# Row sums of x on ScalarE (copies with an accumulator) instead of VectorE, from the third batch on

## The chip, the cores and the metric

The kernel runs on one core of one Trainium2 chip. The metric is the device time of one execution in microseconds; the median of three executions of the kernel before is 617.11 us.

## The reference

A graph attention over 16 batches of 512 nodes with 512 features, two directions (d = 0, 1), 16 heads of 32, and only the first 20 nodes as keys:

```
row_zero = v.sum(-1) == 0                       # per node
q_exp = where(row_zero, 0, q)                   # query features only for nonzero rows
self_feat = concat(v, q_exp) @ W_self.T + b_self
for d in 0, 1:
    A = adj (or its transpose), first 20 keys
    aff = (self_feat Wq)(kv Wk) / sqrt(32), masked where A sums to 0, + A @ w_bias + b_bias
    output += softmax(aff) @ kv, then Wout per head
out = v + relu(output)
```

The change concerns `v.sum(-1)` alone: one sum of 512 float32 values for each of the 512 rows of a batch. The other thing that the sums feed is the test for zero.

## The kernel before

Each engine has its program written out by hand, and semaphores order them. The host gives x twice: `x` with features on partitions, and `xn` with nodes on partitions (512 rows as 128 partitions of 4 rows). For a batch n = b + 1 (next batch) the work is pipelined into batch b:

- SyncE loads `xn`, two rows per partition at a time (`load_rows(b, half)`, 128x1024 values, one buffer), and stores and reloads the zero test as a broadcast row (`store_nonzero`, `load_nonzero`). The row sums run two batches ahead: in batch b they are those of batch b + 2. `load_rows(b + 2, 1)` waits until the first half's sums are done, since there is only one buffer; behind it in SyncE's queue stand `load_c`, `load_x`, `load_mask`, `store_nonzero`, `load_rows(b + 3, 0)` and `load_nonzero`.
- VectorE reduces each half to two columns of `rsum` (`row_sums`, L926 to L928), and `nonzero` (L930 to L934) turns the four sums of a partition into 0 or 1.
- TensorE, per batch: `scores` for four tiles of 128 nodes (L572), `self_feat` of the next batch (L500 to L502, results in PSUM `gen`), the transposes of the softmax weights in five chunks (L584: chunks 0 and 1, then the last `self_feat`, then chunks 2, 3, 4), `attend_rest` (L629) and `attend` 0 to 3 (L500 to L502 into `aff`). In the batches 1, 4, 7, 10 and 13 it also makes the key products of the next group (L540) between the `self_feat` parts. Transposes 2 wait for `wt_low(0)`, transposes 3 for `wt_low(1)`, `attend_rest` for the last `g_low`, the next batch's `scores` for `add_sf(0)` and `add_sf(1)`.
- ScalarE, per batch: `x_high` (L707), the label products (L720) and edge terms (L712 to L716) interleaved with the exp of the four tiles (L880), `sf_high` (L725), in the batches 1, 4, 7, 10, 13 `evict_g` (L737), `evict_wt` of the five chunks (L742), `relu` (L746).
- VectorE, per batch: label sums (L984), `row_sums`, `shift` of each tile (L994, L996), `total` (L1009, L1011), `add_query` (L940), `g_low` (L951) in the batches 1, 4, 7, 10, 13, `row_sums`, `wt_low` 0 and 1 (L956), `nonzero`, `add_query(3)`, `wt_low` 2 to 4, `add_sf` 0 and 1 (L978), `sf_low` (L945), `add_sf` 2 and 3.
- GpSimd, per batch: `x_low` (L1279), `sub_max` (L1298), `normalise_rest` and `normalise` (L1302, L1310), `sf_low` of three chunks (L1283), `bias` of the next batch (L1286, four instructions), and the DMA that adds x to the output (L1321).

"Batch 10" below is the pass of all engines with b = 10. The last use of `row_sums` is in batch 13.

Of the kernel before, what the change touches and what calls it, by code (L numbers as in the profile page):

```python
# [10 lines left out]
ACT = mybir.ActivationFunctionType  # L11
# [34 lines left out]
def build(nc, B, a, out):  # L46
# [4 lines left out]
    with ExitStack() as ctx:  # L51
        def sb(name, shape, dt=F32, stack=ctx):
            return stack.enter_context(nc.sbuf_tensor(name, shape, dt))

        def sem(name):
            return ctx.enter_context(nc.semaphore(name))
# [20 lines left out]
        xn = sb("xn", [P, 2, F])  # L77
        rsum, nzc = sb("rsum", [P, T]), sb("nzc", [P, T])
# [15 lines left out]
        def slots(*held):  # L94
            made = {}
            for k in range(max(len(h) for h in held)):
                with ExitStack() as own:
                    for n, h in enumerate(held):
# [74 lines left out]
        s_xn0, s_xnin, s_rsum, s_nzc, s_nzst, s_nzin = (sem("rows0_in"), sem("rows_in"), sem("row_sums"), sem("nonzero_rows"), sem("nonzero_stored"),  # L173
                                                 sem("nonzero_in"))
# [62 lines left out]
        def upto(b, c):  # L237

            return chunk(b, (LAST_ORDER.index(c) if b == B - 1 else c) + 1)
# [463 lines left out]
        def _(act):  # L703
            def x_high(n):
                act.wait_ge(s_xin, n * 16 + 16)
                for c in range(FC):
                    nc.scalar.activation(xh[:, c, :], x[:, c, :], ACT.Copy).then_inc(s_xh, 1)  # L707

            def edge_terms(n):

                act.wait_ge(s_cond, n + 1)
                nc.scalar.activation(cond[:], cond[:], ACT.Relu).then_inc(s_neg, 1)  # L712
                act.wait_ge(s_neg, n * 3 + 1)
                nc.scalar.activation(cond[:], cond[:], ACT.Relu, scale=-1.0, bias=one[:, 0:1]).then_inc(s_neg, 1)
                act.wait_ge(s_neg, n * 3 + 2)
                nc.scalar.activation(prod[:, :, :, L], cond[:], ACT.Identity, scale=NEG, bias=wb[:, L:L + 1]).then_inc(s_neg, 1)  # L716
# [23 lines left out]
            def evict_wt(b, slot, c):  # L740
                act.wait_ge(s_tp, upto(b, c))
                nc.scalar.activation(wt_high(c), wt_bank(b, c), ACT.Copy).then_inc(s_wth, 1)  # L742
# [114 lines left out]
            def batch(b, slot, i, ahead):  # L857
                n, other = b + 1, 1 - slot
                next_g, pair = next_group(b) is not None, next_group(b)
                if next_g:  # L860
                    k_blocks(pair)
                if ahead >= 1 and b > 0:
                    act.wait_ge(s_sf, b * FC + FC)
                    x_high(n)
                if ahead == 2 and b > 0:
                    act.wait_ge(s_mskin, b * 16 + 48)
                    act.wait_ge(s_vred, b * D + 2 * D)
                    labels(b + 2, range(0, L, LG))
                if ahead == 0:
                    for j in range(HG):  # L870
                        add_bosum(b, slot, j)
                for t in range(T):
                    if next_g and t == T - 1:
                        evict_g(pair, 0)
                        evict_g(pair, 1)
                    if ahead == 0 and t == T - 1:
                        act.wait_ge(s_sub3, 1)
                    else:
                        act.wait_ge(s_sub, b * T + (t + 1))
                    nc.scalar.activation(z[slot][:, t, :], z[slot][:, t, :], ACT.Exp).then_inc(s_exp, 1)  # L880
                    if b == 0 and t == 0:
                        edge_terms(1)
                    if ahead == 2 and b > 0 and t + 1 < LG:
                        labels(b + 2, range(t + 1, L, LG))
                    if ahead == 2 and b > 0 and t + 1 == LG:
                        edge_terms(b + 2)
                if b == 0:
                    act.wait_ge(s_mskin, 48)
                    act.wait_ge(s_vred, 2 * D)
                    labels(2, range(0, L, LG))  # L890
                    sf_high(1, 1, 0)
                    sf_high(1, 1, 1)
                for f in range(FC - 1):
                    if next_g and f >= 1:
                        evict_g(pair, G2 * f)
                        evict_g(pair, G2 * f + 1)
                    if ahead >= 1 and b > 0:
                        sf_high(n, other, f)
                if ahead == 0:
                    for c in LAST_ORDER:  # L900
                        evict_wt(b, slot, c)
                    last_relu(b, slot, 0)
                    return
                evict_wt(b, slot, 0)
                evict_wt(b, slot, 1)
                if b == 0:
                    labels(2, range(1, L, LG))
                    sf_high(1, 1, 2)
                if next_g:
                    evict_g(pair, GU - 2)  # L910
                    evict_g(pair, GU - 1)
                for c in range(2, WC):
                    evict_wt(b, slot, c)
                if ahead >= 1:
                    sf_high(n, other, FC - 1)
                if b == 0:
                    labels(2, range(2, L, LG))
                    edge_terms(2)
                for j in range(HG):
                    relu(b, slot, j)  # L920

            batches(batch)

        @block.vector
        def _(dve):
            def row_sums(n, half, src, s_in, count):  # L926
                dve.wait_ge(s_in, count)
                nc.vector.tensor_reduce(rsum[:, 2 * half:2 * half + 2], src, AX_X, ALU.add).then_inc(s_rsum, 1)  # L928
# [224 lines left out]
            def first_batch(b, slot):  # L1153
                n, other = b + 1, 1 - slot
                shift(b, slot, 0)
                x_low(XP)
                shift(b, slot, 1)
                x_low(XP + 1)
                total(b, slot, 0)
                shift(b, slot, 2)  # L1160
                total(b, slot, 1)
                shift(b, slot, 3)
                dve.wait_ge(s_bx, T)
                label_sum(n, 0)
                label_sum(n, 1)
                dve.wait_ge(s_out[other], 16)
                add_query(n, other, 0)
                total(b, slot, 2)
                total(b, slot, 3)
                add_query(n, other, 1)  # L1170
                row_sums(n + 1, 0, xn[:], s_xnin, 48)
                label_mask(n + 1)
                add_query(n, other, 2)
                wt_low(b, slot, 0)
                wt_low(b, slot, 1)
                add_query(n, other, FC - 1)
                wt_low(b, slot, 2)
                wt_low(b, slot, 3)
                wt_low(b, slot, 4)
                add_sf(b, slot, 0)  # L1180
                add_sf(b, slot, 1)
                sf_low(n, other)
                row_sums(n + 1, 1, xn[:], s_xnin, 64)
                nonzero(n + 1, True)
                for j in range(2, HG):
                    add_sf(b, slot, j)

            def batch(b, slot, i, ahead):
                if b == 0:
                    return first_batch(b, slot)  # L1190
                n, other = b + 1, 1 - slot
                next_g, pair = next_group(b) is not None, next_group(b)
                if b == 1:

                    shift(b, slot, 0)
                    dve.wait_ge(s_bx, b * T + T)
                    label_sum(n, 0)
                    label_sum(n, 1)
                    shift(b, slot, 1)
                    label_mask(b + 2)  # L1200
                    shift(b, slot, 2)
                    total(b, slot, 0)
                    total(b, slot, 1)
                    shift(b, slot, 3)
                    row_sums(b + 2, 0, xn[:], s_xnin, b * 32 + 48)
                else:
                    if ahead >= 1:
                        dve.wait_ge(s_bx, b * T + T)
                        label_sum(n, 0)
                        label_sum(n, 1)  # L1210
                    if ahead == 2:
                        row_sums(b + 2, 0, xn[:], s_xnin, b * 32 + 48)
                    shift(b, slot, 0)
                    if ahead == 2:
                        label_mask(b + 2)
                    shift(b, slot, 1)
                    total(b, slot, 0)
                    shift(b, slot, 2)
                    total(b, slot, 1)
                    if ahead >= 1:  # L1220
                        shift(b, slot, 3)
# [22 lines left out]
                if next_g:  # L1244
                    g_low(pair, 2)
                    g_low(pair, 3)
                    add_query(n, other, 2)
                if ahead == 2:
                    row_sums(b + 2, 1, xn[:], s_xnin, b * 32 + 64)
                if next_g:  # L1250
                    g_low(pair, 4)
                    g_low(pair, 5)
# [184 lines left out]
```

## Time and profile before

| | |
|---|---|
| three runs | 617.08, 617.11, 618.52 us |
| span of the profiled execution | 616.5 us |
| PE, PEld busy | 606.8, 532.3 us |
| DVE, ACT, POOL busy | 527.0, 386.7, 436.2 us |
| granted TensorE clock, mean | 0.998 |

The span runs from the first to the last instruction of the profiled execution; the time of a run, which is measured on the device as a whole, stands 0.6 us above it by the median. PE is TensorE's matmuls, PEld its weight loads, DVE VectorE, ACT ScalarE, POOL GpSimd. SPq is SyncE's queue of DMA issues. Times on the profile are microseconds from the start of the span.

### The profile page before, as it was taken

How to read it: one execution, taken by the hardware profiler on the slowest of the kernel's cores; microseconds unless marked ns; L12 is line 12 of the kernel's file. 1: busy time of each engine (PE TensorE's matmuls, PEld its weight loads, DVE VectorE, ACT ScalarE, POOL GpSimd, SP SyncE). 2: the span in 40 equal slices, each digit the busy share in tenths (PEclk: the TensorE clock that was granted, in tenths of full speed). 3: DMA queues.
4: the chain of work that ended last, by engine and by line, in shares of the span. 5: the costliest groups of instructions: out<-in, count | busy, mean ns of one | idle time of the engine just before them, and what ended most of it. 6: DMA issues, size and time to landing. Idle time of an engine off the chain costs nothing.

```text
span 616.5 us, 10667 instructions
## 1 busy us (share of the span) xinstructions
PE 606.8 (98%) x4047; PEld 532.3 (86%) x4047; DVE 527.0 (85%) x770; ACT 386.7 (63%) x737; POOL 436.2 (71%) x400
## 2 busy tenths in 40 slices
PE   9999999999999999999999999999999999999995
PEld 6977898989898988989898898989898989889892
DVE  4898899999797989989797988888897979787675
ACT  4658647877566776757586755668574758653432
POOL 0301388876978886797986688989569798858852
PEclk9999999999999999999999999999999999999999
DMA  8976545846758672657775385857357676726061
GB/s 312 424 284 183 146 109 172 212 183 128 269 113 270 120 263 52 160 194 175 225 165 192 71 237 154 241 143 207 119 121 262 129 251 127 256 53 169 1 147 69
DMA packets 54466, 109.54 MB, mean 178 GB/s; under 512 B 27855, under 2 KB 37583, under 8 KB 47695
## 3 DMA queue, kind: packets, MB, share of 16 engines
q1 hardware_dynamic: 52254, 93.13, 47.7%
q0 software_dynamic: 2160, 15.73, 14.0%
q8 instruction: 32, 0.52, 0.4%
q14 instruction: 20, 0.16, 0.1%
HBM read 88.05 MB, written 20.78 MB: 177 GB/s over the span
## 4 chain that ended last, share of the span: by engine, by line
PE 94%; DVE 3%; POOL 1%; issue 1%; ACT 0%
PE aff L572 36%; PE gen L500 10%; PE gen L502 9%; PE gen L501 9%; PE aff L540 8%; PE tp L584 4%; PE aff L500 3%; PE aff L502 3%; PE aff L501 3%; PE aff L629 2%; PE gen L584 1%; PE tp L500 1%; PE tp L502 1%; PE tp L501 1%; PE tp L402 1%; DVE wol L1074 1%
## 5 line engine op out<-in xcount | busy, mean ns | idle before, releaser
L572 PE MATMUL aff<-gh,sfl 128*128 128x320 f32 x504 | 114.9, 309 | 0.0
L572 PE MATMUL aff<-gh,sfh 128*128 128x320 f32 x504 | 114.8, 309 | 0.0
L572 PE MATMUL aff<-gl,sfh 128*128 128x320 f32 x504 | 114.8, 309 | 0.0
L1279 POOL TENSOR_TENSOR xl<-x,xh 128x512 fp32r<-128x512 f32 x62 | 84.9, 1424 | 33.5 <-ACT xh L707 33.5
L1286 POOL TENSOR_TENSOR z<-cb,bx 128x640 f32<-128x640 f32 x64 | 100.6, 1607 | 10.7 <-PE tp L502 10.2
L500 PE MATMUL gen<-xh,w1h 128*128 128x512 f32 x256 | 104.0, 406 | 0.0
L502 PE MATMUL gen<-xh,w1l 128*128 128x512 f32 x256 | 100.5, 393 | 0.0
L501 PE MATMUL gen<-xl,w1h 128*128 128x512 f32 x256 | 99.8, 390 | 0.0
L880 ACT ACTIVATE z<-z 128x640 f32<-128x640 f32 x64 | 47.4, 741 | 79.1 <-POOL z L1298 77.2
L1283 POOL TENSOR_TENSOR sfl<-sff,sfh 128x512 fp32r<-128x512 f32 x48 | 61.2, 1293 | 46.0 <-ACT sfh L725 45.8
L1298 POOL TENSOR_TENSOR z<-z,mx 128x640 f32<-128x640 f32 x63 | 81.6, 1295 | 16.3 <-DVE mx L996 16.3
L720 ACT ACTIVATE prod<-msk,wb 128x160 f32<-128x160 int32 x176 | 90.5, 589 | 0.0
L572 PEld LDWEIGHTS aff<-gh,sfh 128*128 128x128 f32 x504 | 84.9, 188 | 1.5 <-DVE sff L978 0.2
L572 PEld LDWEIGHTS aff<-gh,sfl 128*128 128x128 f32 x504 | 84.2, 188 | 0.0
L572 PEld LDWEIGHTS aff<-gl,sfh 128*128 128x128 f32 x504 | 84.2, 188 | 0.0
L1310 POOL TENSOR_TENSOR z<-z,rcp 128x512 f32<-128x512 f32 x63 | 67.0, 1064 | 2.6
L1009 DVE TENSOR_REDUCE rcp<-z 128x32 f32<-128x640 f32 x64 | 51.9, 810 | 15.8 <-ACT z L880 15.7
L994 DVE TENSOR_TENSOR z<-aff,z 128x640 f32<-128x640 f32 x63 | 50.7, 805 | 14.3 <-PE aff L572 14.2
L737 ACT ACTIVATE gh<-aff 128x480 fp32r<-128x480 f32 (+1 forms) x96 | 43.5, 529 | 30.2 <-PE aff L540 29.4
L746 ACT ACTIVATE sff<-sff,bosum 128x512 f32<-128x512 f32 x60 | 40.6, 717 | 33.0 <-DVE sff L978 33.0
L951 DVE TENSOR_TENSOR gl<-aff,gh 128x480 fp32r<-128x480 f32 (+1 forms) x96 | 51.6, 594 | 11.2 <-ACT gh L737 10.6
L725 ACT ACTIVATE sfh<-sff 128x512 fp32r<-128x512 f32 x64 | 40.5, 635 | 29.1 <-DVE sff L940 29.1
(163 smaller groups left out, 1215.3 us busy)
## 6 DMA issues: line engine op xcount, KB each, us to landing
x<-in_x SPq DMA_DIRECT2D x16, 1024.0 KB, 8.6
xn<-in_xn SPq DMA_DIRECT2D x31, 512.0 KB, 5.4
sff<-in_x POOLq DMA_DIRECT2D x15, 1024.0 KB, 8.4
out_y<-sff SPq DMA_DIRECT2D x15, 1024.0 KB, 4.9
msk<-in_mask SPq DMA_DIRECT2D x17, 880.0 KB, 7.4
cb<-c_scratch SPq DMA_DIRECT2D x16, 320.0 KB, 6.9
nz<-nz_scratch SPq DMA_DIRECT2D x16, 256.0 KB, 4.0
wkT<-in_wkT SPq DMA_DIRECT2D x4, 512.0 KB, 8.2
```

What stands on the lines that cost most here:

```text
L500: nc.tensor.matmul(acc, lh, rh, start=first, stop=False)
L501: nc.tensor.matmul(acc, lh, rl, start=False, stop=False)
L502: return nc.tensor.matmul(acc, ll, rh, start=False, stop=last)
L572: mm = nc.tensor.matmul(aff[:, t % 2, half, 0:SH], s, g[:, b - starts[group(b)], f, half * SH:(half + 1) * SH], start=(f == 0 and i == 0), ...
L720: last = nc.scalar.activation(prod[:, :, :, l], msk[:, :, :, :, l].rearrange("p t d m -> p t (d m)"), ACT.Copy, scale=wb[:, l:l + 1])
L951: lo = nc.vector.tensor_tensor(g_part(gl, pair, u, r), g_bank(pair, u, r), g_part(gh, pair, u, r).bitcast(F32), ALU.subtract)
L1009: nc.vector.tensor_reduce(rcp[:, t, :], z[slot][:, t, :].rearrange("p (g m) -> p g m", m=M), AX_X, ALU.add).then_inc(s_sum, 1)
L1279: nc.gpsimd.tensor_tensor(xl[:, c, :], x[:, c, :], xh[:, c, :].bitcast(F32), ALU.subtract).then_inc(s_xl, 1)
L1283: nc.gpsimd.tensor_tensor(sfl[:, f, :], sff[slot][:, f, :], sfh[:, f, :].bitcast(F32), ALU.subtract).then_inc(s_sfl2, 1)
L1286: nc.gpsimd.tensor_tensor(z[slot][:, t, :].rearrange("p (q e) -> p q e", q=QG), cb[:].rearrange("p (q e) -> p q e", q=QG), bx[:, t].rearra ...
L1298: nc.gpsimd.tensor_tensor(zt(slot, t), zt(slot, t), heads(mx, t, M), ALU.subtract).then_inc(s_sub, 1)
L1310: nc.gpsimd.tensor_tensor(z[slot][:, t, 0:HG * P].rearrange("p (g m) -> p g m", m=MA), zt(slot, t)[:, :, 0:MA], heads(rcp, t, MA), ALU.mul ...
```

## The change

The row sums of batches 2 to 15 (made in batches 0 to 13) are taken from VectorE and made by ScalarE. A half of the rows, until now one VectorE reduction, becomes two ScalarE activations: each copies one row per partition onto itself and gives the sum in `accum_out`. The first half's pair stands behind the exp of tile 1 (and the label products that follow it), the second half's pair ahead of `evict_wt(0)`. ScalarE waits for the rows' DMA and for the previous batch's `nonzero` before it writes `rsum`. `nonzero` stays on VectorE and where it was.

```
+            def row_sums(n, half, count):
+                act.wait_ge(s_xnin, count)
+                act.wait_ge(s_nzc, n)
+                for t in range(2):
+                    last = nc.scalar.activation(xn[:, t, :], xn[:, t, :], ACT.Copy, accum_out=rsum[:, 2 * half + t:2 * half + t + 1])
+                last.then_inc(s_rsum, 1)
...
                     if ahead == 2 and b > 0 and t + 1 == LG:
                         edge_terms(b + 2)
+                    if ahead == 2 and t == 1:
+                        row_sums(b + 2, 0, b * 32 + 48)
...
+                if ahead == 2:
+                    row_sums(b + 2, 1, b * 32 + 64)
                 evict_wt(b, slot, 0)
                 evict_wt(b, slot, 1)
...
-                row_sums(n + 1, 0, xn[:], s_xnin, 48)
...
-                row_sums(n + 1, 1, xn[:], s_xnin, 64)
                 nonzero(n + 1, True)
...
                     shift(b, slot, 3)
-                    row_sums(b + 2, 0, xn[:], s_xnin, b * 32 + 48)
...
-                    if ahead == 2:
-                        row_sums(b + 2, 0, xn[:], s_xnin, b * 32 + 48)
                     shift(b, slot, 0)
...
-                if ahead == 2:
-                    row_sums(b + 2, 1, xn[:], s_xnin, b * 32 + 64)
                 if next_g:
                     g_low(pair, 4)
```

## Rows read from the trace of the kernel before

**Rows 1.** The page, busy time by engine: us (share of the span) x instructions.
```profile
PE 606.8 (98%) x4047; PEld 532.3 (86%) x4047; DVE 527.0 (85%) x770; ACT 386.7 (63%) x737; POOL 436.2 (71%) x400
```
**Rows 2.** Chain that ended last: start us, us, what; scores of batches 11, 12, 13.
```profile
451.42 14.08 PE aff L572 x96
...
482.56 14.08 PE aff L572 x96
...
513.92 14.08 PE aff L572 x96
```
**Rows 3.** Waits of PE's weight loads: us in total, times, longest.
```profile
PEld tp L584 <- POOL z L1310: 1.5, 5, 0.5
```
**Rows 4.** Groups by line: xcount | busy us, mean ns | idle before.
```profile
L928 DVE TENSOR_REDUCE rsum<-xn 128x2 f32<-128x1024 f32 x30 | 36.3, 1208 | 0.0
...
L707 ACT ACTIVATE xh<-x 128x512 fp32r<-128x512 f32 x64 | 35.0, 619 | 0.6 <-DMA x<-in_x 0.5
...
L712 ACT ACTIVATE cond<-cond 128x160 f32<-128x160 f32 x16 | 5.2, 324 | 0.0
```
**Rows 5.** Timeline of ACT, batch 10: start us, us, what, xcount [idle before].
```profile
441.26 0.65 ACT L725 ACTIVATE sfh<-sff 128x512 fp32r<-128x512 f32 x1
441.78 1.11 ACT L742 ACTIVATE wth<-tp 128x512 fp32r<-128x512 f32 x2
```
**Rows 6.** Timeline of DVE, batch 10.
```profile
442.78 1.27 DVE L956 TENSOR_TENSOR wtl<-tp,wth 128x512 fp32r<-128x512 f32 x2
443.97 0.82 DVE L934 SCALAR_TENSOR_TENSOR nzc<-rsum,one 128x4 f32<-128x4 f32 x1
444.89 2.35 DVE L951 TENSOR_TENSOR gl<-aff,gh 128x480 fp32r<-128x480 f32 x4
...
449.61 1.28 DVE L978 TENSOR_TENSOR sff<-aff,sff 128x512 f32<-128x512 f32 x2
```
**Rows 7.** Timeline of POOL, batch 10.
```profile
443.24 6.12 POOL L1286 TENSOR_TENSOR z<-cb,bx 128x640 f32<-128x640 f32 x4
```
**Rows 8.** Timeline of PE's weight loads, end of batch 10.
```profile
447.50 0.19 PEld L629 LDWEIGHTS aff<-wth,vr 32*128 32x128 f32 x4 [0.17 <-issue]
...
451.03 0.41 PEld L572 LDWEIGHTS aff<-gh,sfh 128*128 128x128 f32 x2
```
**Rows 9.** Timeline of DVE, batch 11.
```profile
475.72 1.29 DVE L956 TENSOR_TENSOR wtl<-tp,wth 128x512 fp32r<-128x512 f32 x2 [1.18 <-ACT wth L742]
476.92 1.49 DVE L934 SCALAR_TENSOR_TENSOR nzc<-rsum,one 128x4 f32<-128x4 f32 x1
...
480.79 1.27 DVE L978 TENSOR_TENSOR sff<-aff,sff 128x512 f32<-128x512 f32 x2
```
**Rows 10.** Timeline of POOL, batch 11.
```profile
476.83 6.16 POOL L1286 TENSOR_TENSOR z<-cb,bx 128x640 f32<-128x640 f32 x4
```
**Rows 11.** Timeline of PE's weight loads, end of batch 11.
```profile
476.99 1.03 PEld L584 LDWEIGHTS tp<-ident,z 128*128 128x128 f32 x8
...
482.18 0.41 PEld L572 LDWEIGHTS aff<-gh,sfh 128*128 128x128 f32 x2
```
**Rows 12.** Timeline of ACT, batch 9.
```profile
396.00 0.74 ACT L880 ACTIVATE z<-z 128x640 f32<-128x640 f32 x1 [1.69 <-POOL z L1298]
```
**Rows 13.** Timeline of DVE, batch 9.
```profile
404.72 1.29 DVE L956 TENSOR_TENSOR wtl<-tp,wth 128x512 fp32r<-128x512 f32 x2 [1.18 <-ACT wth L742]
405.92 0.69 DVE L934 SCALAR_TENSOR_TENSOR nzc<-rsum,one 128x4 f32<-128x4 f32 x1
```
**Rows 14.** Timeline of SyncE's DMA queue, batch 9.
```profile
391.96 0.43 SPq L268 DMA_DIRECT2D xn<-in_xn  x1
```
**Rows 15.** The page, DMA issues: xcount, KB each, median us to landing.
```profile
x<-in_x SPq DMA_DIRECT2D x16, 1024.0 KB, 8.6
xn<-in_xn SPq DMA_DIRECT2D x31, 512.0 KB, 5.4
```
**Rows 16.** Instructions that write nzc: duration ns min/median/max, first and last start.
```profile
L934 DVE SCALAR_TENSOR_TENSOR nzc<-rsum,one x16: 161/826/1491, 37.6 to 545.6; 128x4 f32<-128x4 f32 x16
```

## The prediction

> **What bounds the kernel now.** I read the page's busy shares first: PE is busy for 606.8 of 616.5 us [rows 1], so at most some 10 us can be won, and what matters is what can make PE late. Then the chain of waits in order of time, for the period of a batch. Batch 11 takes 482.56 - 451.42 = 31.14 us from the start of its scores to the start of the next, batch 12 takes 513.92 - 482.56 = 31.36 us [rows 2]. The second is one of four batches (3, 6, 9, 12) whose first transposes wait for GpSimd's last normalised tile: PE's weight loads wait there 1.5 us in 5 waits, all ahead of L584 [rows 3]. Nearly everything else is PE behind PE. So the steady batches are bound by PE with the other engines close behind it, and the question is how close. I read this from each engine's timeline at the end of a batch, for three kinds of batch: "key" batches (1, 4, 7, 10, 13: they also make the g terms of the next group; batch 10 is read), the batches after them (2, 5, 8, 11; batch 11 is read), and the others (3, 6, 9, 12; batch 9 is read).
>
> **What is removed.** 28 VectorE reductions of 128x1024, two in each of the batches 0 to 13, at 1208 ns [rows 4]: 28 x 1.21 = 33.9 us off VectorE. None lies on PE's chain. The first of a batch stands ahead of the first shift of the scores, the second ahead of add_query(2) or g_low(4), both upstream of idle time of VectorE. What they can give back is the 0.22 us by which batch 12 is longer than batch 11 [rows 2], in four batches: 0.9 us.
>
> **What is added.** 56 ScalarE copies of 128x512 with an accumulator output, in pairs. The trace shows no such instruction, so I bound a pair. The plain copy is L707, 619 ns, and L712, 160 elements wide, takes 324 ns [rows 4]: (619 - 324)/352 = 0.84 ns an element, so 324 - 160 x 0.84 = 190 ns are fixed. Lower end: two copies at 0.52 us, as if the accumulator were free and each overlapped the next by the 0.1 us that sf_high (start 441.26, 0.65 us) shows against evict_wt (start 441.78) [rows 5]: 1.04 us. Upper end: two instructions as long as the exp of 640 elements (0.74 us [rows 12]), each with a narrow one (0.32 us) behind it: 2.1 us. I take a copy without overlap, 0.62, plus the fixed part of one more narrow instruction, 0.19: 0.8 each, **D = 1.6 us a pair**, since writing the sum out must wait for the last element. In all 28 x 1.6 = 45 us more on ScalarE, which has idle time for it. Only the place matters.
>
> **First pair** (after the exp of tile 1 and its labels). The exp of tile 2 waits 1.69 us for GpSimd in batch 9 [rows 12], so a pair of 1.6 us fits; at D = 2.1 the exp is 0.4 us late, and the normalising behind it queues on GpSimd anyway. I count nothing.
>
> **Its DMA.** The load of the second half of the rows waits for the first pair's semaphore, and SyncE's queue holds load_c, load_x and load_mask behind it. Today it leaves at 391.96 in batch 9 [rows 14]. The new place is behind exp(1) and three labels: about 396.00 - 1.69 + 1.6 = 395.9 at the latest, some 4 us later. A rows load lands in 5.4 us by the median [rows 15], so at 401.3; the second pair stands ahead of an eviction that ended as wt_low started, at 404.7 [rows 13], so it wants it at about 404.1. Cover: 2.8 us. Cost nothing, bound in the rivals. The stores of the nonzero rows move later by about a microsecond and are not needed before the next batch.
>
> **Second pair** (ahead of evict_wt(0), where the next engine is VectorE with wt_low(0)). Behind it in ScalarE's queue stand both evictions and, in key batches, evict_g(6) and (7); VectorE's wt_low(0), wt_low(1), nonzero, g_low(6), g_low(7), add_query(3), wt_low(2) to (4), add_sf(0) and (1) wait for them in order; PE waits for wt_low(0) ahead of transposes 2, wt_low(1) ahead of transposes 3, g_low(7) ahead of attend_rest, add_sf(1) ahead of the next scores.
> *Key batches (read in batch 10).* Eviction 0 starts at 441.78 + 1.6 = 443.38 [rows 5], and the first of the two ends 0.6 us later (two take 1.11 us, overlapping by 0.1), so wt_low starts at 444.0 instead of 442.78: 1.2 us late, since VectorE was 0.4 us the later one until now. nonzero would start at 443.97 + 1.2 = 445.2 [rows 6]. Its length depends on GpSimd: it takes 0.82 us here and ends at 444.79, and the first of GpSimd's four bias instructions, 6.12/4 = 1.53 us each from 443.24, ends at 444.77 [rows 7]. The same in batch 11: nonzero ends at 478.41, the first bias at 476.83 + 1.54 = 478.37 [rows 9, 10]. It seems to wait for the running GpSimd instruction to end; it would now catch the second one and end at 446.30 + 0.05, 1.56 us late instead of 1.2. VectorE has no idle time from there to add_sf(1). g_low ends at 447.24 + 1.56 = 448.8, and the weight load of attend_rest started at 447.50: PE stalls 1.3 us; add_sf ends at 450.89 + 1.56 = 452.45 against a load at 451.03 [rows 6, 8]: 1.4 us, the same stall, not another. I take 1.3 for four batches, and 0.6 for batch 13, whose tiles are a third shorter: 5.8 us.
> *Batches after them (read in batch 11).* wt_low(0) waited 1.18 us for the eviction already, so the whole of D arrives at VectorE. wt_low(0) and (1) end at 477.01 + 1.6 = 478.6; PE's transposes 2 and 3 load from 476.99 on, the second half at 477.5 [rows 9, 11]: 1.1 us late. nonzero, from 478.5, would end with the second bias (479.9, or 0.3 us less as GpSimd runs a little ahead): 1.25 to 1.55 us late, against 0.12 us of slack of the scores (482.06 to 482.18). I take 1.1, between: 4.4 us for four.
> *Others (read in batch 9).* add_query(2), ahead of the eviction's queue, no longer stands behind a sum; of its 1.2 us I give the pair 0.2 (an estimate, batch 11 shows nothing of it since add_query waits for PE there). wt_low, which waited 1.18 us for the eviction, starts 1.4 us late, nonzero at 405.92 + 1.4 = 407.3 [rows 13]; GpSimd's chain is up to 1 us earlier here, so whether nonzero catches a bias instruction is open. The slack of transposes 3, 0.5 us as in batch 11, gives a stall of 0.9, a caught bias 1.5. I take 1.0: 4.0 us.
> *Batch 0* has PE idle time of its own, and its second pair runs while ScalarE waits for the transposes; nothing.
>
> Sum: 5.8 + 4.4 + 4.0 - 0.9 = 13.3 us. The span of the profiled execution becomes 616.5 + 13.3 = 629.8; the median of the runs before is 617.11, 0.6 above that span, so **630.4 us**, or 2.2% slower.
>
> **A rule against the trace.** nonzero takes between 161 and 1491 ns for the same four elements a partition [rows 16], and both ends that I checked fall on the end of a GpSimd instruction. The Trainium skill, page "SBUF — State Buffer", section "Who interferes with whom", says why: a VectorE instruction with two inputs in SBUF shares a read interface with GpSimd instructions that read SBUF, and the later one blocks until the earlier one is done. The trace agrees. The skill's page "VectorE: DVE Perf Modes", section "Rules for kernel authors", speaks for the change instead: it calls tensor_reduce the slowest VectorE operation and advises restructuring; by it alone one would subtract VectorE's 33.9 us, which the trace doesn't allow because VectorE isn't what PE waits for at those places.
>
> **Rivals.**
> Rival 1, *only D, no caught instruction*: nonzero runs short (0.16 us) when it starts after a bias has ended. Key batches then lose 445.2 + 0.16 - 444.79 = 0.6 less 0.26 of slack, 0.35; the batches after them 1.1 all the same, by transposes 3; the others 0.9. Sum 5 x 0.35 + 4 x 1.1 + 4 x 0.9 - 0.9 = 8.9: 626 us. With D at 1.04 as well, 0.5 and 0.3 are left in the plain batches and the sum is about 3 to 4: 621 us. For it: which instruction is caught depends on tenths of a microsecond. Chance 0.28.
> Rival 2, *the pair is dearer*: D = 2.1, every plain batch 0.5 us longer, key batches 0.2: 13.3 + 4.0 + 1.0 = 18.3, 635 us. Chance 0.12.
> Rival 3, *the rows land late*: the second load shares the DMA engines with load_c and load_x behind it. If it takes the 8.6 us of an x load [rows 15], it lands at 395.9 + 8.6 = 404.5, 0.4 us behind its need, in eight plain batches: 3 us on top, 634 us. Against it: it stands ahead of x in the queue. Chance 0.06.
> Rival 4, *the other side, faster*: the second pair is covered. It decides in ScalarE's idle time before evict_wt(0): were D below the slack of transposes 3 and of VectorE together (0.5 us in plain batches, 0.4 of VectorE's lateness in key ones), nothing would be lost and the 0.9 us of the four batches won: 616 us. Against it: even two plain copies take 1.04 us. Chance 0.06.
> My forecast has 0.48.
>
> **How the numbers follow.** With about 0.3% (1.9 us) as what a measurement can tell from no change, only rival 4 falls on the faster or the unchanged side; I split it and add a little for covers that I have not seen: faster 0.04, same 0.06, slower 0.90. The range reaches from the low form of rival 1 to rivals 2 and 3: 620 to 637 us.
>
> **What would show it.** Steps right: PE weight loads ahead of L584, L629 and L572 waiting for VectorE's wtl, gl and sff (today 1.5 us for L584, from GpSimd) with 12 to 14 us in all; ScalarE busy by 45 us more; wt_low(0) waiting longer for evict_wt in each batch; nonzero still ending with a GpSimd instruction; periods of about 32.2 and 32.1 us instead of 31.14 and 31.36, and 1.3 us more in key batches. The forecast is wrong if a pair takes under 1.1 us, if nonzero is short in most batches, or if the pair itself waits for its DMA.

## The result and the profile after

The changed kernel takes 630.09 us by the median (629.44 to 632.46, 4 runs) against 617.10 us (617.00 to 618.52, 4 runs): ratio 1.021, 95% interval 1.0188 to 1.0232. The forecast was 630.4 us. The change is slower, clear of the noise; whether by more or less than 2% the interval leaves open.

First, from the trace of the kernel after, the busy time by engine, then the groups of the added instructions (xcount | busy us, mean ns | idle before) and the range of nonzero's durations (min/median/max in ns). They answer to [rows 1, 4, 16].
```profile
PE 611.2 (97%) x4047; PEld 530.5 (84%) x4047; DVE 502.4 (80%) x742; ACT 422.1 (67%) x849; POOL 434.0 (69%) x400
...
L713 ACT ACTIVATE xn<-xn 128x512 f32<-128x512 f32 x56 | 34.6, 622 | 0.0
...
L713 ACT ACTIVATION_READ_ACCUMULATOR xn<-xn 128x1 f32 x56 | 10.8, 192 | 0.0
...
L945 DVE SCALAR_TENSOR_TENSOR nzc<-rsum,one x16: 161/1474/1533, 37.8 to 559.6; 128x4 f32<-128x4 f32 x16
```
Each sum is two instructions: the copy, 622 ns, and one that reads the accumulator, 192 ns. ScalarE is busy 422.1 - 386.7 = 35.4 us longer, not the 45 us of the forecast, because each read overlaps its copy; VectorE is busy only 24.6 us less, although 33.9 us of sums left it, mainly since nonzero grew from a median of 826 to one of 1474 ns (7.2 us in all; some 2 us of the difference stay unexplained).

The chain that ended last, by the starts of the scores of batches 10 to 13, answers to [rows 2].
```profile
421.06 14.31 PE aff L572 x96
...
462.37 14.08 PE aff L572 x96
...
494.33 14.31 PE aff L572 x96
...
526.52 14.31 PE aff L572 x96
```
And from the same view of the kernel before, the start of batch 10:
```profile
411.58 14.08 PE aff L572 x96
```
Batch 10 takes 41.31 us (before 451.42 - 411.58 = 39.84), batch 11 31.96 (31.14), batch 12 32.19 (31.36). The same subtraction over all batches:

| batches | before, us each | after, us each | lost in all | forecast |
|---|---|---|---|---|
| 0 and 1 together | 71.84 | 73.22 | 1.38 | 1.3 |
| 4, 7, 10 | 39.82 to 39.84 | 41.31 to 41.36 | 4.5 | 3.9 |
| 13 | 39.68 | 40.26 | 0.6 | 0.6 |
| 2, 5, 8, 11 | 31.14, 31.15 | 31.95, 31.96 | 3.25 | 4.4 |
| 3, 6, 9, 12 | 31.35, 31.36 | 32.19, 32.20 | 3.35 | 3.1 |
| sum | | | 13.05 | 13.3 |

The split between the kinds depends on where one cuts. Behind a plain batch (one without key products) the chain shows scores of 14.31 us, behind a key batch 14.08, so 0.23 us of what a plain batch loses appears in the period of the next one. From the end of one batch's scores to the end of the next, all eight plain batches take 32.19 or 32.20 us and batch 10 takes (462.37 + 14.08) - (421.06 + 14.31) = 41.08. Counted so, the losses are 1.25 to 1.3 us in each of the batches 4, 7 and 10, 0.35 in batch 13, 1.05 in 2, 5, 8 and 11 and 0.84 in 3, 6, 9 and 12: in all 3.8, 0.35, 4.2 and 3.35 us, each within 0.3 us of its forecast.

The waits of PE's weight loads (us in total, times, longest) answer to [rows 3]; the last line is matmuls.
```profile
PEld aff L629 <- issue: 8.0, 16, 1.4
PEld tp L584 <- DVE wtl L967: 7.2, 16, 0.7
...
PEld aff L572 <- issue: 3.9, 8, 0.5
...
PE aff L629 <- DVE gl L962: 4.9, 5, 1.2
```
The transposes wait for wtl in 16 places, two in each of the eight plain batches; attend_rest waits for gl in the five key batches. "issue" hides the same wait: L629's 2.9 us before have become 8.0, and they are 3.0 again when nonzero is made short (experiment 3). With the 0.5 us still from GpSimd, the weight loads ahead of L584, L629 and L572 wait 19.6 us, 15.0 more than before, where the forecast named 12 to 14; since loads run ahead of their matmuls, not all of it is lost time.

The timeline of batch 10, as in [rows 5 to 8]: ScalarE, VectorE, GpSimd, PE's weight loads (start us, us, what).
```profile
450.97 0.65 ACT L732 ACTIVATE sfh<-sff 128x512 fp32r<-128x512 f32 x1
451.49 0.65 ACT L713 ACTIVATE xn<-xn 128x512 f32<-128x512 f32 x1
452.01 0.22 ACT L713 ACTIVATION_READ_ACCUMULATOR xn<-xn 128x1 f32 x1
452.11 0.65 ACT L713 ACTIVATE xn<-xn 128x512 f32<-128x512 f32 x1
...
452.72 1.10 ACT L749 ACTIVATE wth<-tp 128x512 fp32r<-128x512 f32 x2
```
```profile
453.36 1.29 DVE L967 TENSOR_TENSOR wtl<-tp,wth 128x512 fp32r<-128x512 f32 x2 [0.80 <-ACT wth L749]
454.57 1.48 DVE L945 SCALAR_TENSOR_TENSOR nzc<-rsum,one 128x4 f32<-128x4 f32 x1
455.97 2.34 DVE L962 TENSOR_TENSOR gl<-aff,gh 128x480 fp32r<-128x480 f32 x4
```
```profile
452.95 6.09 POOL L1290 TENSOR_TENSOR z<-cb,bx 128x640 f32<-128x640 f32 x4
```
```profile
458.42 0.22 PEld L629 LDWEIGHTS aff<-wth,vr 32*128 32x128 f32 x4 [1.38 <-issue]
```
The pair takes the place of the eviction from 451.49 to 452.72, which is 1.23 us. wt_low, which used to follow g_low at once, now waits 0.80 us for the eviction. nonzero starts at 454.57, just behind the end of GpSimd's first bias instruction (452.95 + 1.52 = 454.47), and ends at 456.05 with the second (455.99). g_low ends at 458.31, and the load of attend_rest at 458.42 has waited 1.38 us.

### The profile page after: what moved, and what is told of

Its sections match the earlier page's. It is cut to its first block, busy times and chain, and to the rows that moved or that the text cites. A ratio compares the mean times of both kernels' runs of the same rounds, so it can differ in the third digit from the quotient of the medians.

```text
span 628.1 us, 10779 instructions
## 1 busy us (share of the span) xinstructions
PE 611.2 (97%) x4047; PEld 530.5 (84%) x4047; DVE 502.4 (80%) x742; ACT 422.1 (67%) x849; POOL 434.0 (69%) x400
## 4 chain that ended last, share of the span: by engine, by line
PE 77%; DVE 10%; ACT 6%; DMA 4%; issue 2%; POOL 1%; SPq 0%
PE aff L572 33%; PE gen L500 7%; PE gen L502 7%; PE gen L501 7%; PE aff L540 5%; PE aff L500 3%; ACT xn L713 3%; PE aff L502 3%; PE aff L501 3%; PE aff L629 2%; PE tp L584 2%; DVE wtl L967 2%; DVE gl L962 2%; DMA sff<-in_x 2%; DVE nzc L945 1%
## 5 line engine op out<-in xcount | busy, mean ns | idle before, releaser
L572 PE MATMUL aff<-gh,sfh 128*128 128x320 f32 x504 | 115.4, 310 | 0.7
L572 PE MATMUL aff<-gh,sfl 128*128 128x320 f32 x504 | 114.8, 309 | 0.0
L572 PE MATMUL aff<-gl,sfh 128*128 128x320 f32 x504 | 114.8, 309 | 0.0
L1283 POOL TENSOR_TENSOR xl<-x,xh 128x512 fp32r<-128x512 f32 x62 | 87.1, 1459 | 33.7 <-ACT xh L707 33.7
L1290 POOL TENSOR_TENSOR z<-cb,bx 128x640 f32<-128x640 f32 x64 | 98.5, 1573 | 10.2 <-PE tp L502 10.2
L1302 POOL TENSOR_TENSOR z<-z,mx 128x640 f32<-128x640 f32 x63 | 83.8, 1330 | 8.4 <-DVE mx L1007 8.4
L572 PEld LDWEIGHTS aff<-gh,sfh 128*128 128x128 f32 x504 | 84.3, 188 | 4.6 <-issue 3.9
L572 PEld LDWEIGHTS aff<-gl,sfh 128*128 128x128 f32 x504 | 84.2, 188 | 0.0
L572 PEld LDWEIGHTS aff<-gh,sfl 128*128 128x128 f32 x504 | 84.2, 188 | 0.0
L951 DVE SCALAR_TENSOR_TENSOR sff<-nz,qb,gen 128x512 f32<-128x512 f32 x64 | 46.8, 732 | 28.4 <-PE gen L502 27.0
```

The lines of the kernel that those rows point to most:

```text
L572: mm = nc.tensor.matmul(aff[:, t % 2, half, 0:SH], s, g[:, b - starts[group(b)], f, half * SH:(half + 1) * SH], start=(f == 0 and i == 0), ...
L1283: nc.gpsimd.tensor_tensor(xl[:, c, :], x[:, c, :], xh[:, c, :].bitcast(F32), ALU.subtract).then_inc(s_xl, 1)
L1290: nc.gpsimd.tensor_tensor(z[slot][:, t, :].rearrange("p (q e) -> p q e", q=QG), cb[:].rearrange("p (q e) -> p q e", q=QG), bx[:, t].rearra ...
L1302: nc.gpsimd.tensor_tensor(zt(slot, t), zt(slot, t), heads(mx, t, M), ALU.subtract).then_inc(s_sub, 1)
```

## The experiments

Each was compared with runs of the kernel before on the same chip; the diffs are against the changed kernel unless said otherwise.

**1. Only the first pair on ScalarE.**
```
-                if ahead == 2:
-                    row_sums(b + 2, 1, b * 32 + 64)
                 evict_wt(b, slot, 0)
...
+                if ahead == 2:
+                    row_sums(b + 2, 1, xn[:], s_xnin, b * 32 + 64)
```


> The first pair of copies stays on ScalarE, the second half's sums go back to VectorE where they were. Theory (the whole cost sits in the second pair, ahead of the weight evictions): 616 to 617.5 us, no different from before, with TensorE's weight loads not waiting for wt_low or g_low. Rival (the first pair delays the exp of tile 2 and with it the softmax chain): a good part of the 13 us stays, 620 us or more.


Measured: 616.52 us against 616.99, ratio 0.9998 (0.9987 to 1.0009). As the theory had it: 28 copies on ScalarE at this place cost nothing. In the trace no transpose waits for wtl in the plain batches any more, and batches 3, 6, 9 and 12 take 31.12 to 31.14 us: their 0.22 us each are won.

**2. Only the second pair on ScalarE.** The first half's sums are back on VectorE at their three old places.
```
-                    if ahead == 2 and t == 1:
-                        row_sums(b + 2, 0, b * 32 + 48)
```


> The first half's sums go back to VectorE, the second pair stays on ScalarE ahead of the evictions. Theory: all of the cost is left, 629 to 631 us, periods of 41.3 us in key batches and 32.0 to 32.2 us in the others. Rival (first pair costs): clearly below 628 us.


Measured: 630.98 us against 616.99, ratio 1.023 (1.0216 to 1.0244). The total is what was expected, but it is made otherwise. ScalarE's timeline in batch 0:
```profile
99.51 0.63 ACT L713 ACTIVATE xn<-xn 128x512 f32<-128x512 f32 x1 [5.07 <-DMA xn<-in_xn]
```
With the first sum late on VectorE, the second load is late and ScalarE waits 5.07 us for it with the evictions behind it. This is what rival 3 of the forecast feared, rows that land late, but for another reason (the load left late, at 94.93) and in one batch only; batches 0 and 1 together take 78.21 us, against 71.84 before. From the scores of batch 2 to those of batch 14 this kernel takes 568.44 - 150.67 = 417.77 us, the changed one 566.78 - 145.94 = 420.84, the one before 553.60 - 144.43 = 409.17. The lines, of this kernel, of the changed one and of the one before:
```profile
150.67 14.07 PE aff L572 x96
...
568.44 14.08 PE aff L572 x96
```
```profile
145.94 14.07 PE aff L572 x96
...
566.78 14.08 PE aff L572 x96
```
```profile
144.43 14.08 PE aff L572 x96
...
553.60 14.08 PE aff L572 x96
```
So the second pair alone costs 8.6 us there and taking the first sum off VectorE, which alone costs nothing, adds 3.1 to it. The timelines of batch 11 show how (VectorE, GpSimd):
```profile
491.52 0.37 DVE L943 SCALAR_TENSOR_TENSOR nzc<-rsum,one 128x4 f32<-128x4 f32 x1
```
```profile
490.32 6.13 POOL L1292 TENSOR_TENSOR z<-cb,bx 128x640 f32<-128x640 f32 x4
```
GpSimd begins its bias instructions together with wt_low(0) (490.32), and nonzero ends with the first one, after 0.37 us. In the changed kernel they begin 0.4 us ahead of wt_low(0) (487.49 against 487.89), so nonzero just misses the end of the first and waits for the second, 1.48 us:
```profile
487.89 1.29 DVE L967 TENSOR_TENSOR wtl<-tp,wth 128x512 fp32r<-128x512 f32 x2 [2.41 <-ACT wth L749]
489.10 1.48 DVE L945 SCALAR_TENSOR_TENSOR nzc<-rsum,one 128x4 f32<-128x4 f32 x1
```
```profile
487.49 6.13 POOL L1290 TENSOR_TENSOR z<-cb,bx 128x640 f32<-128x640 f32 x4
```
The wait of wt_low(0) for the eviction, 1.18 us in [rows 9], is 2.41 us here: the whole of the pair arrives at VectorE. The periods of the plain batches are 31.8 us here and 31.96 and 32.19 there; counted to the end of the scores it is 31.8 against 32.19 in all eight, and a key batch takes 41.1 us in both, where nonzero is held for 1.5 us in both. Nearly all of the 3.1 us is therefore this hold in eight batches. Through which instructions the shorter VectorE program lets GpSimd begin earlier was not followed.

**3. nonzero replaced by a memset.**
```
-                nc.vector.scalar_tensor_tensor(nzc[:], rsum[:], 0.0, one[:], ALU.not_equal, ALU.mult).then_inc(s_nzc, 1)
+                nc.vector.memset(nzc[:], 1.0).then_inc(s_nzc, 1)
```


> The changed kernel with the test for zero left out: nzc is set to 1.0 by a VectorE memset, which reads nothing from SBUF, at the same place and behind the same waits. Theory (nonzero, with two SBUF inputs, waits for GpSimd's running instruction, 1.48 us in most batches): in key batches the chain to the last g_low is only 0.3 to 0.4 us late instead of 1.2, so the stall falls from 1.5 to about 0.2 us (5 x 1.3 less); in the other batches the wait of transposes 3, about 0.6 of 0.82 us, stays; about 622 us. Rival (cost is ScalarE's delay alone, and nonzero would be late anyway): 628 to 630 us.


Measured: 621.37 us against 616.99, ratio 1.0074 (1.0061 to 1.0088): 8.7 of the 13 us are gone. Duration of nonzero, and the chain's starts of the scores of batches 10, 11 and 12:
```profile
L945 DVE MEMSET nzc<- x16: 62/62/62, 37.5 to 551.4; 128x4 f32 x16
```
```profile
414.97 14.08 PE aff L572 x96
...
454.86 14.08 PE aff L572 x96
...
486.67 14.08 PE aff L572 x96
```
A key batch takes 39.89 us, 0.05 above before, a plain one 31.81. What is left is 0.67 us in each of the batches after the key ones and 0.45 in batches 3, 6, 9 and 12 (0.67 less the 0.22 won). It goes with the wait of the transposes for wtl, still 7.2 us in 16 times in this trace.

**4. The second pair moved to where ScalarE idles.**
```
                     if ahead >= 1 and b > 0:
                         sf_high(n, other, f)
+                    if ahead == 2 and f == 1:
+                        row_sums(b + 2, 1, b * 32 + 64)
...
-                if ahead == 2:
-                    row_sums(b + 2, 1, b * 32 + 64)
                 evict_wt(b, slot, 0)
```


> The second pair moved ahead in ScalarE's order: behind sf_high(1) instead of ahead of evict_wt(0). ScalarE is idle there for 2.1 us (batch 9) and 2.5 us (batch 10) and the pair takes 1.22 us. Theory: no delay of the evictions, no stall, 616 to 617.2 us, 0 to 0.9 us below before because VectorE's relief ends GpSimd's wait in batches 3, 6, 9 and 12. Rival 1 (the rows, which are requested only about 8 us ahead, land late there): sf_high(2) late, above 619 us. Rival 2 (extra ScalarE work costs wherever it stands): above 625 us.


Measured: 615.81 us (11 runs) against 616.99, ratio 0.9979 (0.9966 to 0.9991): 0.2% better than the kernel before, and only just clear of the noise. In batch 10 ScalarE makes the pair while TensorE works on the key products:
```profile
436.87 0.65 ACT L713 ACTIVATE xn<-xn 128x512 f32<-128x512 f32 x1
437.40 0.22 ACT L713 ACTIVATION_READ_ACCUMULATOR xn<-xn 128x1 f32 x1
437.49 0.65 ACT L713 ACTIVATE xn<-xn 128x512 f32<-128x512 f32 x1
438.01 0.22 ACT L713 ACTIVATION_READ_ACCUMULATOR xn<-xn 128x1 f32 x1
439.48 1.96 ACT L744 ACTIVATE gh<-aff 128x480 fp32r<-128x480 f32 x4 [1.25 <-PE aff L540]
```
and is idle for 1.25 us even after it. Batches 11 and 12 take 31.15 and 31.12 us: the 0.22 us by which batch 12 was the longer one before are won, four times. That is 0.9 us; experiments 1 and 5 win the same in their traces, and their medians don't differ from before.

**5 and 6. The length of what stands ahead of the eviction.** The second half as one copy of a single element (5), and as one of its two rows (6).
```
-                for t in range(2):
+                for t in range(2) if half == 0 else ():
...
+                if half == 1:
+                    last = nc.scalar.activation(xn[:, 0, 0:1], xn[:, 0, 0:1], ACT.Copy)
```
```
-                for t in range(2):
+                for t in (0, 1) if half == 0 else (1,):
```


> The sums of the second half are left out from batch 2 on: the second pair becomes one ScalarE copy of a single element, with the same waits and semaphore (about 0.2 us ahead of the evictions instead of 1.22). Theory (only the length of what stands ahead of evict_wt counts, from a slack of about 0.5 us on): 616 to 617 us. Rival (the waits and semaphores at that place cost, not the length): above 620 us.

> Half of the second pair is left out (one row of the two): 0.61 us ahead of the evictions. Theory (a threshold: 0.5 us of slack of transposes 3 in plain batches, 0.4 us of VectorE's lateness in key ones, and nonzero then starts before GpSimd's first bias instruction ends): 616.5 to 618.5 us, that is at most 0.1 to 0.2 us a batch. Rival (cost proportional to the length): 623 to 624 us.


Measured: 616.73 us against 616.89 (0.9992, 0.9977 to 1.0007) and 617.07 us (0.9997, 0.9985 to 1.0009). With one row ahead, 0.61 us, a key batch takes 39.82 us and the plain ones 31.18 to 31.21, that is 0.05 us more than with the tiny copy (31.12 to 31.15). With two rows, 1.23 us, it is 1.5 and 0.8 us. So the cost isn't proportional to the length: it begins near 0.6 us. How it grows from there to 1.23 us no run shows.

**7 and 8. What holds nonzero.** In 7 the test for zero is left out (nzc gets the sum itself), in 8 it is made with two constants in place of the second input.
```
+                nc.vector.tensor_reduce(nzc[:], rsum[:].unsqueeze(2), AX_X, ALU.max).then_inc(s_nzc, 1)
...
+                nc.vector.tensor_scalar(nzc[:], rsum[:], 0.0, 1.0, ALU.not_equal, ALU.mult).then_inc(s_nzc, 1)
```


> The changed kernel with nonzero's test left out: it is a VectorE tensor_reduce over an axis of one element, which reads rsum from SBUF (one input) and writes nzc. Theory (an instruction with one SBUF input and no two-port mode isn't held by GpSimd): as with the memset, about 0.1 us long, 621 to 622 us. Rival (any VectorE instruction that reads SBUF is held by GpSimd's, and the memset was short because it reads nothing): about 1.4 us long and 629 to 631 us.

> The changed kernel with nonzero as a tensor_scalar with two immediates (not equal 0, times 1): one SBUF input, the same result. By the Trainium skill, page SBUF — State Buffer, section Who interferes with whom, such an instruction enters a two-port mode and is held all the same: about 1.4 us long, 628 to 631 us. Rival (one input is enough to escape): about 0.1 us long, 621 to 622 us. No trace so far shows which.


Measured: 621.66 us against 616.89 (1.0074, 1.0053 to 1.0096) and 629.60 us (1.0211, 1.018 to 1.0241). The durations (min/median/max ns), of 7 and of 8:
```profile
L945 DVE TENSOR_REDUCE nzc<-rsum x16: 145/146/157, 37.7 to 551.9; 128x4 f32<-128x4 f32 x16
```
```profile
L945 DVE TENSOR_SCALAR nzc<-rsum x16: 170/1486/1542, 38.1 to 559.5; 128x4 f32<-128x4 f32 x16
```
Both read the same four values from SBUF. The reduction is not held in any of its 16 executions (145 to 157 ns), the tensor_scalar is held like the instruction with two inputs (median 1486 ns). The Trainium skill says just this on its page "SBUF — State Buffer", section "Who interferes with whom": a reduction never contends with GpSimd on this chip, a tensor_scalar can, by entering a two-port mode. The durations agree; that the two-port mode is the reason, no run here shows.

**9. The second pair behind the first two evictions.**
```
                 evict_wt(b, slot, 0)
                 evict_wt(b, slot, 1)
+                if ahead == 2:
+                    row_sums(b + 2, 1, b * 32 + 64)
```


> The second pair stands behind evict_wt(1) instead of ahead of evict_wt(0); the transposes' evictions are then on time. Theory (what counts next is who waits for the sums: nonzero stands in VectorE's order right behind wt_low(1), so VectorE now waits about 1.2 us for them, and in key batches evict_g(6) and (7) are behind the pair too): the wait of transposes 3 is gone, but the last g_low and add_sf(1) are as late as before, about 1 us or more in each of the 13 batches; 626 to 632 us. Rival (the order of the evictions alone matters): 616 to 618 us.


Measured: 617.33 us against 617.13, ratio 1.0004 (0.9992 to 1.0016). The theory's number was a miss. VectorE in batch 11, then GpSimd:
```profile
476.71 1.29 DVE L967 TENSOR_TENSOR wtl<-tp,wth 128x512 fp32r<-128x512 f32 x2 [1.18 <-ACT wth L749]
478.42 0.70 DVE L945 SCALAR_TENSOR_TENSOR nzc<-rsum,one 128x4 f32<-128x4 f32 x1 [0.42 <-ACT xn L713]
```
```profile
477.54 6.15 POOL L1290 TENSOR_TENSOR z<-cb,bx 128x640 f32<-128x640 f32 x4
```
The pair doesn't begin when VectorE is done with wt_low: it starts at 477.06, while VectorE still works on it, so VectorE waits 0.42 us and not 1.2. And nonzero would have been held until 477.54 + 1.54 = 479.08 in any case; it ends at 479.12. The hold absorbs the wait. The place isn't quite free in the trace: batches 0 and 1 together take 73.21 us (before 71.84) and each key batch 0.1 us more, which the 0.22 us won in four batches make up in part.

**10. The kernel before with the memset** (the diff of 3, against the kernel before).


> The kernel before with nonzero's test left out (a memset of 1.0 at its place). Its nonzero takes 0.8 to 1.5 us there. Theory (in the kernel before VectorE's chain has 0.1 to 0.3 us of slack to TensorE, so what nonzero gives back isn't wanted): 616 to 617.2 us, no difference. Rival (the hold of nonzero costs in the kernel before too): 1 us or more below.


Measured: 616.71 us against 617.13, ratio 0.9994 (0.9977 to 1.0011): no difference. In the kernel before the hold costs nothing; it costs only once VectorE is late.

## Why the prediction was right, step by step

- *Nothing on the removed side but 0.9 us.* Experiments 1, 4 and 5: batches 3, 6, 9 and 12 become as short as the others (31.12 to 31.14 us), and no more than that.
- *The length of a pair.* The mis-sized term: D was put at 1.6 us and is 1.23 (451.49 to 452.72). The narrow instruction was there and as long as estimated, 0.19 us, but it starts 0.1 us before its copy ends and the next copy starts 0.1 us after it has started, so each sum occupies 0.61 us. The forecast's reason for no overlap, that the read must wait for the last element, doesn't show in these records.
- *The first pair costs nothing.* Experiment 1. What the prediction lacked is that it changes the second pair's price, by 3.1 us (experiment 2), since with VectorE relieved GpSimd's bias instructions begin 0.4 us or more earlier against wt_low.
- *Its DMA is covered.* Of ScalarE's waits for a DMA in the changed kernel's trace none is for the rows. The forecast had the load of batch 9 leave some 4 us later than before; it leaves 2.1 us later behind the start of the scores (402.69 - 388.86 = 13.83 us, before 391.96 - 380.22 = 11.74):
```profile
402.69 0.35 SPq L268 DMA_DIRECT2D xn<-in_xn  x1
```
In experiment 2 such a wait lasted 5.07 us in batch 0.
- *The second pair.* Experiments 1, 4, 5 and 9 each take it away from ahead of evict_wt(0) and each gives the whole 13 us back. The two ways that the sum had are both there: the transposes' wait for wt_low alone is 0.67 us in the batches after the key ones (experiment 3) where 1.1 was taken, because D was too long; the hold of nonzero is the rest, 8.7 us. In key batches 1.3 us was taken and 1.25 to 1.3 is lost, counted to the end of the scores: nonzero is held by the second bias instruction, as forecast.
- *What was luck.* Without a caught bias instruction the forecast's own rival 1 comes to 8.9 us, so 4.4 of its 13.3 us were the hold. Measured it is the other way round: 621.37 - 616.99 = 4.4 us without the hold, and 8.7 from it. In plain batches D was 0.37 us too long, and the hold, which was counted there only as one end of a range, made up for it: 1.05 us against the 1.1 and 1.0 taken.
- *That a short D would nearly do away with the cost* (rival 1's low form, 621 us at D = 1.04, and rival 4 below 0.5 us): up to 0.61 us it does (experiment 6); a D of 1.04 was not run. Rival 1's other half, that no bias is caught, is what experiments 3 and 7 measure: 621.4 and 621.7 us, where it said 626 at the D of 1.6.
- *The sum against the median.* The 0.6 us between span and median was a coincidence: the changed kernel's runs lie 1.7 to 1.9 us above their own spans, so the profiled execution of before was probably (an estimate) the run of 618.52 us, not one of the median. The profiled execution of before had its last four stores issued in 3.98 us, the one after in 2.21 us:
```profile
609.72 3.98 SPq L393 DMA_DIRECT2D out_y<-sff  x4
```
```profile
622.90 2.21 SPq L393 DMA_DIRECT2D out_y<-sff  x4
```
The spans thus differ by 11.6 us and the medians by 13.0; the sum over the batches, 13.05, is the one that fits. Why those stores were slower is open; in all eleven other traces they take 2.2 us.

The mechanism and the places were thus right, and the total of 13.3 against 13.05 us looks more exact than the sizes of its two causes were.

## What to carry to other kernels

Whether moved work is free is decided by what is queued behind it at its new place, not by the engine's busy share: the same pair costs 13 us ahead of an eviction, and nothing 5 us earlier or right behind the second one. On a kernel that is bound by one engine, relieving another wins only the waits that the bound engine shows. And a tiny VectorE instruction can be as long as a GpSimd instruction; look at the spread of durations of one group, not at its mean, and give it a form that isn't held or a place where GpSimd rests.

## What the runs showed of the hardware

An accumulator output costs ScalarE a second instruction of 192 ns for a 128x512 copy of 622 ns; in a row, a copy and its read take 0.61 us. VectorE's four-element nonzero took 0.16 to 1.54 us in the forms with two SBUF inputs and as tensor_scalar, 0.15 us as a reduction and 0.06 us as a memset, beside the same GpSimd work. In plain batches a VectorE program shorter by one reduction made it longer (0.35 to 0.59 us in experiment 2, 1.47 to 1.48 us in the changed kernel), as GpSimd's instructions began 0.4 to 0.65 us earlier against wt_low.
